# Fused attention and RWKV feed-forward block on one core: the order of a step on TensorE, the split of the score banks, and the place of half the value projections

## Time and profile before

| | |
|---|---|
| median of 3 runs | 1705.68 us |
| the profiled execution | 1697.48 us |
| its span, first to last instruction | 1695.8 us |
| PE / VectorE / ScalarE / POOL busy | 86 / 67 / 55 / 37% |
| mean granted clock of PE | 0.877 |
| PE waits for VectorE before row units | 75.1 us, 123 times |
| PE waits for ScalarE before column units | 7.7 us, 25 times |
| PE waits for POOL before dense units (mix_lo, k_lo) | 29.0 and 15.0 us |

### The profile page before, as it was taken

The page is one execution under the profiler, slowest core; times in us unless marked ns, Lnnn a source line. Parts: engine busy times, 40 slices in busy tenths (PEclk is TensorE's granted clock), DMA queues, the critical chain, the costliest instruction groups (busy, mean ns, idle before and its releaser), DMA issues.

```text
span 1695.8 us, 30093 instructions
## 1 busy us (share of the span) xinstructions
PE 1451.8 (86%) x10856; PEld 824.9 (49%) x10856; DVE 1132.3 (67%) x2246; ACT 927.1 (55%) x1859; POOL 622.5 (37%) x752
## 2 busy tenths in 40 slices
PE   3699898889998999899898999899898999988653
PEld 2354445544554545545454545545454545544343
DVE  4567566877778677867778777877778677774330
ACT  2046555566556555666556555666565555556321
POOL 3002112343334433443334433443335333333454
PEclk7688779989998889989898899989998999988765
DMA  3121113221232123211231123212231113220200
GB/s 106 45 64 44 44 46 96 70 52 47 71 93 54 43 55 103 70 52 49 66 95 51 43 58 109 64 52 58 70 91 45 49 54 89 59 58 20 71 7 19
DMA packets 79828, 102.96 MB, mean 61 GB/s; under 512 B 22576, under 2 KB 43320, under 8 KB 79680
## 3 DMA queue, kind: packets, MB, share of 16 engines
q1 hardware_dynamic: 76544, 91.86, 19.9%
q0 software_dynamic: 2560, 8.39, 1.3%
q10 hardware_dynamic: 576, 0.79, 0.2%
HBM read 31.74 MB, written 8.94 MB: 24 GB/s over the span
## 4 chain that ended last, share of the span: by engine, by line
PE 60%; DVE 17%; ACT 7%; POOL 7%; issue 7%; DMA 1%; SPq 0%; ACTq 0%; POOLq 0%; DVEq 0%
PE val_ps L1136 14%; PE col_ps L1067 12%; PE row_ps L1104 11%; PE dense_ps L1146 8%; DVE max_a L876 7%; PE dense_ps L1147 5%; PE dense_ps L1148 5%; ACT weights L714 3%; PE row_ps L1115 3%; PE dense_ps L1165 2%; POOL mix_lo L655 1%; DVE xn_a L912 1%; DVE max_b L876 1%; POOL weights L603 1%; DVE mixed L975 1%
## 5 line engine op out<-in xcount | busy, mean ns | idle before, releaser
L714 ACT ACTIVATE weights<-col_ps 128x512 f32<-128x512 f32 (+2 forms) x1280 | 633.6, 559 | 445.3 <-PE col_ps L1067 443.8
L876 DVE TENSOR_REDUCE max_a<-row_ps 128x1 f32<-128x512 f32 (+3 forms) x896 | 538.7, 644 | 212.5 <-PE row_ps L1115 124.6
L1104 PE MATMUL row_ps<-k_stack,q_stack 62*128 62x512 f32 (+3 forms) x1536 | 406.8, 438 | 88.9 <-DVE max_a L876 75.1
L1067 PE MATMUL col_ps<-q_stack,k_stack 64*128 64x512 f32 (+3 forms) x1536 | 394.9, 444 | 8.1 <-ACT weights L714 7.7
L1136 PE MATMUL val_ps<-weights,v_ones 128*32 128x512 f32 (+3 forms) x3072 | 359.3, 543 | 26.8 <-POOL weights L603 24.1
L603 POOL TENSOR_SCALAR_AFFINE_SELECT weights<-weights 128x512 f32<-128x512 f32 x256 | 165.3, 646 | 564.5 <-ACT weights L714 564.1
L876 DVE TENSOR_REDUCE max_b<-row_ps 128x1 f32<-128x384 f32 (+3 forms) x384 | 215.2, 595 | 160.3 <-PE row_ps L1115 157.5
L1104 PEld LDWEIGHTS row_ps<-k_stack,q_stack 62*128 62x128 f32 x1536 | 200.4, 205 | 241.0 <-DVE max_a L876 152.0
L1067 PEld LDWEIGHTS col_ps<-q_stack,k_stack 64*128 64x128 f32 x1536 | 191.2, 203 | 231.7 <-ACT weights L714 156.2
L1115 PE MATMUL row_ps<-mask_fill,mask_ident 64*128 64x64 bf16 (+1 forms) x2048 | 151.2, 219 | 0.0
L1136 PEld LDWEIGHTS val_ps<-weights,v_ones 128*32 128x32 f32 x3072 | 63.2, 112 | 121.4 <-issue 64.1
(11 more groups left out here) (123 smaller groups left out, 2114.5 us busy)
## 6 DMA issues: line engine op xcount, KB each, us to landing
q_stack<-q_part SPq DMA_DIRECT2D x384, 64.0 KB, 2.2
k_stack<-k_part SPq DMA_DIRECT2D x372, 64.0 KB, 2.2
xa<-in_x SPq DMA_DIRECT2D x8, 1024.0 KB, 7.0
att<-val_out SPq DMA_DIRECT2D x64, 128.0 KB
recips<-recip_rows SPq DMA_DIRECT2D x32, 256.0 KB
xq<-in_x SPq DMA_DIRECT2D x28, 256.0 KB, 3.3
out<-xq POOLq DMA_DIRECT2D x28, 256.0 KB, 2.6
q_stack<-max_rows SPq DMA_DIRECT2D x256, 4.0 KB
```

Source lines behind the costliest of these rows:

```text
L714: nc.scalar.activation(weights[:, t % 2, heads[0]:heads[-1] + 1:2, 0:q1 - q0], col_ps[bank][:, 0:n * (q1 - q0)].rearrange("p (h q) -> p h ...
L876: nc.vector.reduce_max(dest, bank[:, 0:len(heads) * (k1 - k0)].rearrange("p (h k) -> p h k", h=len(heads)), AX_X).then_inc(max_done, 1)
L1067: last = nc.tensor.matmul(col_ps[bank][:, i * (q1 - q0):(i + 1) * (q1 - q0)], stack_at(k_stack[s % 2], rows, heads[i], P * j, P * (j + 1)) ...
L1104: last = nc.tensor.matmul(banks[odd][:, n * width:(n + 1) * width], stack_at(q_stack[stack], rows, heads[n], P * i, P * (i + 1)), stack_at ...
```

## The change

PE's step becomes: all row units, first column pair, values of the step before, dense units, second column pair. In steps 1, 2, 9 and 10, where there is a dense unit, it goes ahead of the values. The row units have four banks, the column units two. Two of the four "v" units go from steps 1 and 9 of s=0 to steps 7 and 9 of s=3 of the batch before; ScalarE's evacuation follows, with waits that the old values have been used. VectorE's order follows PE's: two maxima with the evacuations between them, the rest of q or k, the other maxima, both halves of the mix. In the first stage, ScalarE's key copies are issued ahead of s=3's steps and not after them.

```diff
+COL_BANKS, ROW_BANKS = 2, 4
...
-V_STEPS, QK_STEPS, T_STEPS = (0, 1, 3, 9), (4, 5, 7, 8), (3, 5, 7, 9)
+V_EARLY, V_STEPS, QK_STEPS, T_STEPS = (7, 9), (0, 3), (4, 5, 7, 8), (3, 5, 7, 9)
...
+SELECT_LATE = (1, 2, 9, 10)
...
-        col_ps = [ps(f"col_ps{i}", [P, HALF]) for i in range(3)]
-        row_ps = [ps(f"row_ps{i}", [P, HALF]) for i in range(3)]
+        col_ps = [ps(f"col_ps{i}", [P, HALF]) for i in range(COL_BANKS)]
+        row_ps = [ps(f"row_ps{i}", [P, HALF]) for i in range(ROW_BANKS)]
...
-        def bank_of(position, period):
+        def bank_of(position, period, banks):
 
-            if position >= 3:
-                return position % 3, 3
-            last = max(p for p in range(period) if p % 3 == position)
+            if position >= banks:
+                return position % banks, banks
+            last = max(p for p in range(period) if p % banks == position)
             return position, position + period - last
...
                 if t in V_STEPS:
-                    k = V_STEPS.index(t)
+                    k = 2 + V_STEPS.index(t)
                     return "v", k, b * 4 + (k + 1)
...
+            if s == G - 1 and fronts(kind) and t in V_EARLY:
+                k = V_EARLY.index(t)
+                return "v", k, b * 4 + (4 + k + 1)
...
-        def row_groups(t):
+        def row_group(t):
 
             first = sum(PER_STEP[:t])
-            units = list(range(first, first + PER_STEP[t]))
-            return units[:2], units[2:]
+            return list(range(first, first + PER_STEP[t]))
...
@@ ScalarE
-                        wait(act, val_done, val_index(b, 0, 0))
+                    last_use = val_index(b, 0, 0) if k >= 2 else val_index(b, G, 0)
+                    wait(act, val_done, last_use - (6 - 2 * k if k < 3 else 0))
...
+                    if kind == "first" and (s, t) == (G - 1, 0):
+                        fill_first_keys()
...
-            pipeline(nc.scalar, body, fill_first_keys)
+            pipeline(nc.scalar, body)
...
@@ VectorE
-                    early, late = row_groups(t) if has_rows(kind, s) else ([], [])
+                    units = row_group(t) if has_rows(kind, s) else []
                     if t == 0 and attends(kind):
                         maximum(b, s - 1, MT1)
-                    for u in early[:1]:
+                    for u in units[:1]:
+                        maximum(b, s, u)
+                    for item in at:
+                        empty_dense(*item)
+                    for u in units[1:2]:
                         maximum(b, s, u)
                     rest_of_qk(b, kind, s, t)
-                    for item in at:
-                        empty_dense(*item)
-                    for u in early[1:]:
+                    for u in units[2:]:
                         maximum(b, s, u)
                     for item in at:
                         mix(*item, 0)
-                    for u in late:
-                        maximum(b, s, u)
-                    for item in at:
                         mix(*item, 1)
                         back(*item)
...
@@ TensorE
-                    early, late = row_groups(t) if has_rows(kind, s) else ([], [])
...
+                    backward = [item for item in at if back_unit(*item)]
+                    late_values = t in SELECT_LATE and (unit or backward)
+
+                    row_scores(b, s, row_group(t) if has_rows(kind, s) else [])
                     for c in cols[:1]:
                         score_columns(b, s, t, c)
-                    if attends(kind) if t else has_late(kind, s):
+                    if not late_values and (attends(kind) if t else has_late(kind, s)):
+                        values(*last)
+                    if unit:
+                        claim_dense()
+                        front(unit)
+                    for item in backward:
+                        claim_dense()
+                        back(*item)
+                    if late_values and attends(kind):
                         values(*last)
                     for c in cols[1:]:
                         score_columns(b, s, t, c)
-                    row_scores(b, s, late)
-                    if unit:
-                        claim_dense()
-                        front(unit)
-                    for item in at:
-                        if back_unit(*item):
-                            claim_dense()
-                            back(*item)
```

More of the change, by code:

```diff
@@ L712, in exps @@
                     wait(act, val_done, val_index(b, s, t) - 1)
-                bank, _ = bank_of(COLS * s + c, COLS * G)
+                bank, _ = bank_of(COLS * s + c, COLS * G, COL_BANKS)
                 nc.scalar.activation(weights[:, t % 2, heads[0]:heads[-1] + 1:2, 0:q1 - q0],
@@ L864, in maximum @@
                 at = unit_index(b, s, u)
-                bank = row_ps[bank_of(UNITS * ((s + 1) % G) + u, UNITS * G)[0]]
+                bank = row_ps[bank_of(UNITS * ((s + 1) % G) + u, UNITS * G, ROW_BANKS)[0]]
                 dve.wait_ge(rows_ready, at + 1)
@@ L1062, in score_columns @@
                     for odd, heads in enumerate(pair):
-                        bank, ago = bank_of(COLS * s + c + odd, COLS * G)
+                        bank, ago = bank_of(COLS * s + c + odd, COLS * G, COL_BANKS)
                         if i == 0:
@@ L1074, in row_bank @@
             def row_bank(b, s, u):
-                number, ago = bank_of(UNITS * ((s + 1) % G) + u, UNITS * G)
+                number, ago = bank_of(UNITS * ((s + 1) % G) + u, UNITS * G, ROW_BANKS)
                 wait(pe, max_done, unit_index(b, s, u) + (1 - ago))
@@ L1238, in body @@
                     cols = range(COL_FIRST[t], COL_FIRST[t + 1], 2) if attends(kind) else ()
-                    early, late = row_groups(t) if has_rows(kind, s) else ([], [])
                     last = (b, s, t - 1) if t else (b - 1, G - 1, STEPS - 1) if s == 0 else (b, s - 1, STEPS - 1)
                     unit = front_unit(b, kind, s, t)
-                    row_scores(b, s, early)
+                    backward = [item for item in at if back_unit(*item)]
+                    late_values = t in SELECT_LATE and (unit or backward)
+                    row_scores(b, s, row_group(t) if has_rows(kind, s) else [])
                     for c in cols[:1]:
                         score_columns(b, s, t, c)
-                    if attends(kind) if t else has_late(kind, s):
+                    if not late_values and (attends(kind) if t else has_late(kind, s)):
[7 more added lines that the diff above has]
+                    if late_values and attends(kind):
                         values(*last)
```

## The result

The changed kernel takes **1977.47 us** (median of 4 runs, 1975.48 to 1981.47) against 1705.18 us: a ratio of 1.1605, 95% interval [1.1576, 1.1635]. The loss is 272 us. The forecast had the sign and the places, with 140 us, and its range ended at 1,915.

A forecast was written before the change was run, and what follows sets the result against it. TensorE's in-order queue, 86% busy, was taken to set the time. Groups s=2, 0, 3 and 1 (+7.0, +6.4, +6.2, -0.5) gave +19.1 us a batch, +140 in all: 1846 us, range 1,715 to 1,915.

The forecast's parts named there:

- steps 0 and 1: In s=2, value unit waits for k_lo, with values and second pair now behind it: step 2 starts 1.8 us later.
- step 2: In s=2, the out unit waits for o_lo, no longer hidden by rows, columns and values: +1.7 us.
- steps 3 and 4: In s=2, VectorE catches up while PE stands in step 2, so 9.0 us becomes 7.5: -1.5 us.
- steps 5 to 9: In s=2, five passages between steps wait for both column banks, +3.3 us, and values wait for POOL's select, +0.6.
- steps 10 and 11: In s=2, mix_lo comes 3.4 us after step 9's last pair, and the values that covered it follow the unit: +1.1.
- the chains: Waits for k_lo, o_lo and mix_lo lose their cover in steps 1, 2 and 10: +1.8, +1.7 and +1.1 us in s=2.
- rival 1: Faster: four row banks remove the row waits and the unit between column pairs hides the exponentials; 1,615 us, chance 0.12.
- the passages: From a step's second column pair to the next step's first, PE waits for both column banks: +3.3 us a group.
- I take this share as unchanged: Clock: 30 of 191 us a batch at 1.2 GHz stay, as much added idle is chain time where slower PE costs nothing.
- rival 3: The clock falls with the change: slow time doubles, 12 us a batch over seven, 1,930 us; chance 0.15.
- They take in what the change adds: Group s=1: its existing waits and slow clock, 8.6 us over s=2, absorb the added 7.9: -0.5 us.
- the sign of being right: In the profile after, groups s=0, 2 and 3 would last 51 to 54 us.

The follow-up runs named there:

- kernel with the low part last: Changed kernel with value, out and receptance units doing the 16 matmuls on high parts first, then waiting for the low part: 1860.09 us.
- the one late in steps 1 and 2: Changed kernel with values behind the dense unit in steps 1 and 2 only, values first in steps 9 and 10: 1933.23 us.
- the banks alone: Kernel before with two column banks and four row banks, its order untouched: 1690.84 us, ratio 0.9924.
- filling the waits alone: Changed kernel with 9, 6 and 4 extra matmuls ahead of the waits for k_lo, o_lo and mix_lo: 1923.51 us.
- all rows first: Changed kernel with dense units behind the second column pair, values ahead of both, rows still all first: 1741.90 us, against 1690.66 with banks and move.

## Why the prediction was right and wrong

Step by step, the worked group s=2 (58.3 us after, 45.1 before) answers to the forecast like this; the bounds are the first matmuls of the steps' rows in both traces:

| s=2 | forecast | measured | what the trace shows |
|---|---|---|---|
| steps 0 and 1 | +1.8 | +3.6 | unit at 0.50 of the clock: 2.8 us for 1.5; values 1.3 for 1.0 |
| step 2 | +1.7 | +1.9 | unit at full clock here |
| steps 3 and 4 | -1.5 | +0.7 | clock 0.69 where it was 0.81 |
| steps 5 to 9 | +3.9 | +4.1 | five passages, clock 0.98 |
| steps 10 and 11 | +1.1 | +2.9 | wait of 1.62 us, then unit at 0.50 |
| sum | +7.0 | +13.1 | |

**Right: the chains.** Each came as worked: the value unit at pair + 5.8 us (5.6), 2.52 us of wait; low waits up by 139 us, where the terms of steps 1, 2 and 10 (1.8, 1.7, 1.1) would come to 138 if all of 30 groups had them. (The forecast itself gave s=0 less in step 1 and nothing in s=1, and a wait is not the same as a later start, so the closeness of the two sums is partly chance.) Row waits nearly vanished and rival 1 was out. The kernel with the low part last shows that PE waited for the low parts themselves, the one late in steps 1 and 2 that two thirds of the late values' cost lie in steps 1 and 2.

**Right: the passages, though not in their form.** I gave 3.3 us a group as waits for both banks. In s=2 the first pair of steps 5 to 9 waits 0.26, 0, 0.17, 0.40 and 0.21 us and then runs one matmul after the other, 0.49 us more than a pair issued together: 3.5 us in all. The second half of this counts as busy time, so column waits rose only from 0.5 to 6.3 us a batch (20 waits, 0.32 each), where I had asked for over 10. Over the whole kernel column waits rose by 44.9 us and the busy time on `col_ps` by 74 (469.3 against 394.9), part of it clock; 3.3 us over 30 groups is 99. The price belongs to two banks in this order: the banks alone, with rows and a dense unit in the passage, are part of a gain.

**Wrong: "I take this share as unchanged".** This is the step that failed. The clock's share was taken as fixed, on the ground that added idle is chain time in which a slower PE costs nothing. The chain time costs nothing; what follows it does. Behind the wait for k_lo PE works at 1.2 GHz every time, in the receptance and out units in 32 of 55 cases, and it does the unit and the values behind it at that rate with nobody else late. Slow time went from 31.5 to 65.4 us a batch, which is up to 17 us a batch; filling the waits alone gave back 54 us. That was rival 3, at 0.15. With its 12 us a batch it stood at 1,930.

**Wrong: s=1, "They take in what the change adds".** -0.5 was forecast, +6.9 came (53.8 to 60.7). I let nearly all waits and slow clock of that group be taken in by the new waits. They were not: its clock went from 0.84 to 0.78, it waits 2.52 us for k_lo like the others, and 2.61 for o_lo where it waited 0.92 before and the others wait 1.6. With half of slow time taken off, the four groups grew by 8.0, 8.3, 5.3 and 2.1 us (s=2, 3, 0, 1), 23.7 a batch against 19.1 forecast. So of the 21.6 us a batch that the forecast missed, about 17 are the clock and 2.6 this term. The groups s=2, 3 and 0 last 58.3, 54.6 and 58.2 us, where 51 to 54 were to be the sign of being right.

**Wrong: the gain in steps 3 and 4.** The -1.5 contained the return of the clock to full speed. The two steps took 9.8 us after, at 0.69, where 7.5 were forecast and 9.1 stood before at 0.81 (kernel after, s=2, steps 3 and 4, then 5 to 9):

```profile
865.08:874.86 9.78, 8.77 (x53) 4.95 (x51) 6.65 (x15) 1.74 (x4) 4.37 (x7) 0.69 0.08 28
874.86:896.40 21.54, 19.95 (x120) 8.94 (x116) 14.16 (x26) 13.47 (x27) 1.69 (x2) 0.98 0.15 38
```

The second row is the stretch that was full before (17.4 us by the same bounds, at 1.00): 4.1 us longer, 3.9 forecast (3.3 for the passages and 0.6 for the select), nearly all at full clock.

**The sum of the loss.** The profiled spans differ by 283.9 us: 137 are idle time of PE, 147 busy time. The idle part is accounted for to 1 us: low waits +139, column waits +45, transposes of the maxima +18, dense units behind a bank that ScalarE reads into h_hi +16 (most of it the receptance unit of s=1), rows -68 (-63 for `max_a`), select -14. The busy part is the same matmuls at a lower clock and pairs that run one after the other; how it splits between the two was not measured.

**The penalty rule.** The Trainium skill's penalty (TensorE: Matmul & The Clock Gate, Terms: throttled time times one half) gives an estimate of (633 - 417) / 2 = 108 us of the 272. The runs bound the clock's part from below only, by the 54 us that came back when the waits were filled, so they neither confirm the rule nor contradict it.

**Open.** Why all rows first costs 51 us with the same sum of large waits was not tried further; three quarters of it are busy time of the same matmuls. Open too is why a wait of 2.61 us leaves the out unit of s=1 at full rate and one of 1.62 the receptance unit of s=2 at half.

## What to carry to other kernels

Before moving a unit forward in a queue written by hand, write down what its last operand waits for, and count the work behind it that used to cover that wait. A wait on TensorE can have two prices, its length and half-speed work after it (here in 59 of 82 units, up to 1.3 us a unit): count both, and treat the clock as a result of the change and not as a constant. If such a wait can't be moved, start the part of the product that doesn't need the late operand, or put throwaway matmuls into it. Where such waits are short, as with the banks alone and the order of before, the first of these brought nothing.

## What the hardware showed that was not expected

- Throwaway matmuls pay: some 520 more matmuls on record, 54 us less time, clock 0.840 to 0.889. In the last stage of the kernel with the banks alone they raised the clock from 0.59 and 0.54 to 0.80 and 0.81 and made the kernel 9 us faster.
- A wait of 2.5 us was followed by a unit at half rate 27 times out of 27, one of 2.6 us at another place in the step by a unit at full rate every time: the clock after a wait was to be read from the trace, place by place, and not from the length of the wait.
- Two matmuls on different rows of the array, which run together in 0.50 us, take 0.99 when their banks come free 0.5 us apart, and the profile shows the difference as busy time and not as a wait.
- Two column banks were enough: with rows and a dense unit between the pairs, giving the third to the row units is worth 0.8%.
